# Gates ahead of the last division, logits in two parts, inverse roots on GpSimd, two row turns and four stores moved

## The reference

```
x = x + tanh(g_xattn[0]) * longconv(ctx, ctx, layernorm(x))
x = x + tanh(g_ffn[0])   * routed_lora(layernorm(x))
x = x + tanh(g_xattn[1]) * cross_attention(layernorm(x), ctx)    # 16 heads, int8 fake-quantized projections
x = x + tanh(g_ffn[1])   * moe(layernorm(x))

def layernorm(x): return (x - mean(x)) / sqrt(var(x) + 1e-5)
def moe(x):                                  # 1024 rows of 256
    scores = sigmoid(x @ gate.T)             # 8 experts
    sel = top_k(scores + expert_bias, 2);  s = scores[sel]
    for e in experts: out += silu((s*x) @ w1[e].T) * ((s*x) @ w3[e].T) @ w2[e].T   # rows that chose e
    out += silu(x @ sw1.T) * (x @ sw3.T) @ sw2.T                                    # the shared expert
```

## Time and profile before

| | us |
|---|---|
| median of 3 runs | 219.38 |
| lowest, highest | 218.35, 220.81 |
| the profiled execution | 219.23 |
| its span in the profile | 217.1 |

### The profile page before, as it was taken

The page is one execution under the profiler, slowest core; times in us unless marked ns, Lnnn a source line. Parts: engine busy times, 40 slices in busy tenths (PEclk is TensorE's granted clock), DMA queues, the critical chain, the costliest instruction groups (busy, mean ns, idle before and its releaser), DMA issues.

```text
span 217.1 us, 3560 instructions
## 1 busy us (share of the span) xinstructions
PE 175.5 (81%) x1156; PEld 110.6 (51%) x1156; DVE 167.6 (77%) x465; ACT 101.7 (47%) x256; POOL 81.8 (38%) x114
## 2 busy tenths in 40 slices
PE   0369999989989989885877777887777839989972
PEld 0236555558555556442555556555556417645531
DVE  0798989994178999979889999999957963585634
ACT  2440343211423244642376667776865574553621
POOL 1486557034755540583220204221220195056100
PEclk9999999999999999999599999999999988999998
DMA  6989880000000000000000000000000057456772
GB/s 170 404 232 377 339 268 1 3 0 0 0 0 2 3 2 0 0 0 2 3 0 3 2 0 3 0 3 0 5 0 3 2 97 145 86 97 119 159 170 97
DMA packets 22624, 15.16 MB, mean 70 GB/s; under 512 B 17648, under 2 KB 21328, under 8 KB 22096
## 3 DMA queue, kind: packets, MB, share of 16 engines
q1 hardware_dynamic: 21968, 13.94, 23.4%
q10 hardware_dynamic: 640, 1.02, 1.3%
HBM read 9.68 MB, written 1.07 MB: 50 GB/s over the span
## 4 chain that ended last, share of the span: by engine, by line
PE 40%; DVE 29%; DMA 13%; issue 10%; ACT 3%; SPq 2%; POOL 1%; DVEq 0%; POOLq 0%
DMA R<-R 8%; PE PS L1303 5%; PE PS L1305 5%; PE PS L1304 5%; DVE R L1019 5%; DVE SM L1010 4%; DMA X<-x 4%; PE PS L1391 4%; PE PS L1367 3%; PE PS L1325 3%; PE PS L1630 2%; PE PS L1334 2%; DVE T_R L948 2%; PE PS L1648 2%; PE PS L1579 2%
## 5 line engine op out<-in xcount | busy, mean ns | idle before, releaser
L495 POOL TENSOR_SCALAR R<-QT,SM 128x256 bf16<-128x256 f32 x32 | 16.3, 524 | 26.2 <-DVE SM L1087 19.8
L1256 DVE TENSOR_TENSOR R<-R,PS 128x512 bf16<-128x512 f32 (+1 forms) x17 | 11.7, 686 | 15.8 <-ACT R L761 8.7
L1630 PE MATMUL PS<-R 128*128 128x512 bf16 x64 | 17.5, 395 | 3.5 <-DMA R<-R 3.5
L1010 DVE TENSOR_REDUCE SM<-PS 128x8 f32<-128x1024 f32 x16 | 18.8, 1214 | 1.9 <-PE PS L1454 1.2
L1477 PE MATMUL PS<-CON,R 128*128 128x128 f32 x128 | 19.2, 283 | 1.2 <-ACT R L640 1.2
L471 POOL TENSOR_TENSOR R<-R,CON 128x256 f32<-128x256 f32 x16 | 9.6, 622 | 24.9 <-PE PS L1466 15.7
L640 ACT ACTIVATE R<-PS 128x512 f32<-128x512 f32 x32 | 18.3, 593 | 1.6 <-PE PS L1477 1.4
L1019 DVE TENSOR_TENSOR R<-PS,SM 128x1024 f32<-128x1024 f32 x16 | 18.9, 1215 | 0.0
L336 POOL TENSOR_TENSOR R<-CT 128x512 f32<-128x512 f32 x12 | 13.7, 1142 | 12.5 <-PE PS L1305 7.2
L548 ACT ACTIVATE LNV<-MV,EPSC 128x1 f32<-128x1 f32 (+1 forms) x26 | 7.5, 290 | 22.7 <-DVE MV L933 11.2
L761 ACT ACTIVATE R<-PS 128x512 f32<-128x512 f32 x17 | 10.1, 595 | 14.2 <-PE PS L1630 14.2
(11 more groups left out here) (151 smaller groups left out, 413.0 us busy)
## 6 DMA issues: line engine op xcount, KB each, us to landing
WST<-w SPq DMA_DIRECT2D x3, 1024.0 KB, 11.4
T_R<-lagged SPq DMA_DIRECT2D x2, 768.0 KB, 7.9
X<-x SPq DMA_DIRECT2D x2, 512.0 KB, 6.7
CT<-ctxr SPq DMA_DIRECT2D x1, 1024.0 KB, 7.2
y<-X SPq DMA_DIRECT2D x8, 128.0 KB, 1.9
WKV<-wkv SPq DMA_DIRECT2D x1, 512.0 KB, 9.7
WQP<-wqp ACTq DMA_DIRECT2D x1, 512.0 KB, 6.4
R<-sw SPq DMA_DIRECT2D x3, 128.0 KB, 4.4
```

Of the source, the lines that this page charges most:

```text
L495: nc.gpsimd.tensor_scalar(XB[:, u % XS, j, :], MX[:, b, :], GG[:, b, e:e + 1], 1.0, ALU.mult, ALU.mult).then_inc(e_xb, 1)
L1010: V_.tensor_reduce(MX1[:, b % 2, 8 * c:8 * c + 8], S4[:, 8 * c:8 * c + 8, :], AX.X, ALU.max).then_inc(a_mx, 1)
L1630: ins = M(PS[:, 2 + 2 * (v % 2) + n, :], lhs, rhs, start=(k == 0), stop=(k == NL - 1))
```

## The change

The first group's gates move ahead of block 7's division on VectorE, and block 4's rows behind both. Group 0's logits are made in two parts (three blocks, then the fourth) in another part of bank 6. The gate is a Tanh for both groups now (0.5 tanh(0.5 x) + 0.5, the same sigmoid), so that the addition and the reciprocal go. The inverse roots of blocks 4 to 7 are made by GpSimd, by an addition and a power of -0.5. Block 3's inverse root and rows stand earlier. The transposes of blocks 6 and 7 go from before expert 0 into units 1 and 2. Stores 0 to 3 are issued from ScalarE's queue in units 13 to 16. Group 1's logits and gates move by one unit and in other pieces. The diff without the declarations and a few unchanged lines:

```diff
@@ -318,7 +320,7 @@
         LATE = 3
-        MGT = 2 * GT + 4
+        MGT = 2 * GT + 3
@@ -361,8 +363,9 @@
-        GE_AT = 3
+        GE_AT = 4
+        LOG = 512 - GT * NE
         TC = [0, 2, 4, 10, NH0]
@@ -370,7 +373,7 @@
-            return MGT * (g + 1) - g
+            return MGT * (g + 1)
@@ -424,8 +427,6 @@
                              XB[:, u % XS].rearrange("p j d -> p (j d)"), transpose=True).then_inc(e_td[u % XS], 16)
-                if u >= NG * NE - GT:
-                    store(u - (NG * NE - GT))
             for b in range(GT, NB):
@@ -481,6 +483,13 @@
                 nc.gpsimd.tensor_tensor(X[:, b, :], Y[:, b % 2, :], XPB[:, b, :], ALU.add).then_inc(x3, 1)
+            def late_rstd(b):
+                pool.wait_ge(m_ln, 2 * (b + 1))
+                nc.gpsimd.tensor_scalar(LNV[:, b:b + 1], MV[:, b, 1:2], EPS, None, ALU.add).then_inc(m_rp, 1)
+                pool.wait_ge(m_rp, 2 * (b - GT) + 1)
+                nc.gpsimd.tensor_tensor(RS[:, b:b + 1], LNV[:, b:b + 1], HALFM[:, 0:1], ALU.pow).then_inc(m_rp, 1)
@@ -527,9 +536,15 @@
                 finish(b)
+            late_rstd(GT)
             expert_rows(0)
+            late_rstd(GT + 1)
             expert_rows(1)
-            for u in range(2, NG * NE):
+            expert_rows(2)
+            late_rstd(GT + 2)
+            expert_rows(3)
+            late_rstd(GT + 3)
+            for u in range(4, NG * NE):
                 expert_rows(u)
@@ -678,11 +693,8 @@
                     act.wait_ge(m_gt, gates_done(g - 1))
-                logits = PS[:, 6, 0:GT * NE].rearrange("p (b n) -> p b n", b=GT)
-                if g == 0:
-                    nc.scalar.activation(GE[:, :, :], logits, ACT.Exp, scale=-1.0).then_inc(m_ge, 1)
-                else:
-                    nc.scalar.activation(GE[:, :, :], logits, ACT.Tanh, scale=0.5).then_inc(m_ge, 1)
+                logits = PS[:, 6, LOG:LOG + GT * NE].rearrange("p (b n) -> p b n", b=GT)
+                nc.scalar.activation(GE[:, :, :], logits, ACT.Tanh, scale=0.5).then_inc(m_ge, 1)
@@ -762,34 +774,28 @@
             a_exp(NB - 1, 0)
+            m_rstd(NB - 5)
             o_q_(NB - 3)
             a_exp(NB - 1, 1)
-            m_rstd(NB - 5)
             a_exp(NB - 1, 2)
             o_ev_(NB - 3)
+            m_zt_(NB - 5)
             a_exp(NB - 1, 3)
-            m_zt_(NB - 5)
             o_y_(NB - 3)
             o_pe_(NB - 1)
             o_q_(NB - 2)
-            m_rstd(NB - 4)
+            m_ge_(0)
             o_ev_(NB - 2)
-            m_ge_(0)
             o_y_(NB - 2)
             m_zt_(NB - 4)
+            last_rows(0)
             o_q_(NB - 1)
-            m_rstd(NB - 3)
+            last_rows(1)
             o_ev_(NB - 1)
+            silu(0)
             o_y_(NB - 1)
-            last_rows(0)
-            last_rows(1)
             m_zt_(NB - 3)
-            m_rstd(NB - 2)
-            m_rstd(NB - 1)
-            silu(0)
-            m_zt_(NB - 2)
             last_rows(2)
-            m_zt_(NB - 1)
             last_rows(3)
@@ -799,6 +805,12 @@
                     last_rows(expert(v + XS))
+                if v in (1, 2):
+                    m_zt_(NB - 3 + v)
+                if UNITS - 1 - GT <= v < UNITS - 1:
+                    b = v - (UNITS - 1 - GT)
+                    act.wait_ge(x4, b + 1)
+                    act.dma_start(out[b], X[:, b, :]).then_inc(stored, 16)
             v = UNITS - 1
@@ -1056,7 +1068,10 @@
             def m_rows(b):
-                dve.wait_ge(m_rs, 2 * (b + 1))
+                if b < GT:
+                    dve.wait_ge(m_rs, 2 * (b + 1))
+                else:
+                    dve.wait_ge(m_rp, 2 * (b - GT + 1))
                 V_.tensor_scalar(MX[:, b, :], X[:, b, :], MV[:, b, 0:1], RS[:, b:b + 1], ALU.subtract, ALU.mult
@@ -1064,16 +1079,9 @@
                 s.wait()
-                if k == 0 and g == 1:
+                if k == 1:
                     dve.wait_ge(m_ge, g + 1)
                     s.mark(V_.tensor_scalar(GS[:, :, :], GE[:, :, :], 0.5, 0.5, ALU.mult, ALU.add))
-                elif k == 1 and g == 1:
-                    return
-                elif k == 0:
-                    dve.wait_ge(m_ge, g + 1)
-                    s.mark(V_.tensor_scalar(GE1[:, :, :], GE[:, :, :], 1.0, None, ALU.add))
-                elif k == 1:
-                    s.mark(V_.reciprocal(GS[:, :, :], GE1[:, :, :]))
                 elif k == 2:
@@ -1193,10 +1201,10 @@
-            dve.wait_ge(ones_s, 3)
+            dve.wait_ge(ones_s, 4)
+            m_rows(NB - 5)
             o_norm(NB - 2, 0)
-            m_rows(NB - 5)
             o_norm(NB - 2, 1)
@@ -1204,33 +1212,32 @@
             for k in range(3, 6):
                 o_norm(NB - 2, k)
             finish(NB - 3)
+            m_gates(0, 1)
+            m_gates(0, 2)
+            m_gates(0, 3)
             o_norm(NB - 1, 0)
-            m_rows(NB - 4)
+            m_gates(0, 4)
             o_norm(NB - 1, 1)
-            m_stats(NB - 3, 0)
+            m_gates(0, 5)
             o_norm(NB - 1, 2)
-            m_stats(NB - 3, 1)
+            third_rows(0)
             for k in range(3, 6):
                 o_norm(NB - 1, k)
+            third_rows(1)
+            m_rows(NB - 4)
+            m_stats(NB - 3, 0)
             finish(NB - 2)
+            m_stats(NB - 3, 1)
             m_stats(NB - 2, 0)
-            m_gates(0, 0)
-            m_gates(0, 1)
             m_stats(NB - 2, 1)
-            m_gates(0, 2)
-            m_gates(0, 3)
+            third_rows(2)
+            finish(NB - 1)
             m_rows(NB - 3)
-            m_gates(0, 4)
-            m_gates(0, 5)
-            third_rows(0)
-            third_rows(1)
-            finish(NB - 1)
             m_stats(NB - 1, 0)
             m_stats(NB - 1, 1)
+            third_rows(3)
             m_rows(NB - 2)
-            third_rows(2)
             m_rows(NB - 1)
-            third_rows(3)
             for v in range(UNITS):
@@ -1255,9 +1262,12 @@
-                if GE_AT < v <= GE_AT + 3:
-                    m_gates(1, 2 * (v - GE_AT - 1))
-                    m_gates(1, 2 * (v - GE_AT - 1) + 1)
+                if v == GE_AT + 1:
+                    for k in range(1, 4):
+                        m_gates(1, k)
+                if v == GE_AT + 2:
+                    for k in range(4, 6):
+                        m_gates(1, k)
                 if v >= 1 and (v + XS) % (NE + 1) and v + XS < UNITS:
@@ -1570,15 +1580,17 @@
-            def m_logits(g):
+            def m_logits(g, lo, hi):
                 if g == 0:
                     pe.wait_ge(L["gate"], 16)
-                pe.wait_ge(m_zt, GT * (g + 1))
-                for j in range(GT):
+                pe.wait_ge(m_zt, GT * g + hi)
+                for j in range(lo, hi):
                     for k in range(NL):
-                        ins = M(PS[:, 6, NE * j:NE * j + NE], MZT[:, g, k, P * j:P * j + P], GW[:, k, :],
+                        at = LOG + NE * j
+                        ins = M(PS[:, 6, at:at + NE], MZT[:, g, k, P * j:P * j + P], GW[:, k, :],
                                 start=(k == 0), stop=(k == NL - 1))
-                ins.then_inc(m_gl, 1)
+                if hi == GT:
+                    ins.then_inc(m_gl, 1)
@@ -1660,6 +1672,7 @@
             o_rows(NB - 2)
+            m_logits(0, 0, GT - 1)
             o_transpose(NB - 3)
@@ -1667,9 +1680,9 @@
                 a_values(NB - 1, k)
+            m_logits(0, GT - 1, GT)
             o_transpose(NB - 2)
             o_rows(NB - 1)
-            m_logits(0)
             o_project(NB - 2)
@@ -1677,9 +1690,7 @@
             m_transpose(NB - 3)
-            m_transpose(NB - 2)
             e_hidden(1, 0)
-            m_transpose(NB - 1)
             e_hidden(1, 1)
@@ -1687,8 +1698,10 @@
                 e_out(v - 1)
+                if v in (1, 2):
+                    m_transpose(NB - 3 + v)
                 if v == GE_AT - 1:
-                    m_logits(1)
+                    m_logits(1, 0, GT)
```

5 lines of the change are left out of this document (4 added, 1 removed).

## The result

The changed kernel takes 224.3 us (median of 4 runs, 222.97 to 224.62). Beside it the kernel before took 220.09 (median of 4, 218.35 to 222.32). The ratio is 1.0175, with a 95% interval of 1.0127 to 1.0223: longer, clear of the noise, though the interval does not say whether by more or less than 2%. Ratios here leave out the executions that fell in the chip's slower state, medians and spreads keep them. The forecast was 220.2 with a range of 217.6 to 222.0, which is no clear change, so the measured time lies outside the range. The chain that it described (the stall ahead of block 4's transpose, the low clock, block 7's chain) is there; several of its terms were mis-sized, all to the same side.

What follows compares the result with a forecast made beforehand. It took the chain of waits to bound the tail: GpSimd's rows and a DMA transpose before expert 0, then TensorE, last the sync queue. 219.23 + 2.05 (front, with clock) - 1.0 (stores) = 220.3, stated as 220.2; range 217.6 to 222.0.

Steps and rivals of the forecast that it cites:

- Part 1: Group 0's gates: written at 170.2 instead of 173.0, 2.8 us earlier, with a new 1.28 us table load before the Tanh.
- Part 2: Work behind the gates: block 4's rows end at 172.0, 4.5 us later; expert 0 starts at 178.8 against 177.89.
- The clock's term: TensorE's clock falls in a 3.2 us stall before block 4's transpose; shared expert's first half and transpose take 1.2 us longer.
- The rival "the clock stays up": TensorE's stall before block 4's transpose, 3.2 us against 3.9, does not lower the clock: 219.1 us; chance 0.27.
- Part 3: Inverse roots by power on GpSimd: 0.3 us per power, between 0.2 and 0.75; expert 1 at 182.8 instead of 182.37.
- +0.35 for block 7's transpose: On TensorE, block 7's transpose, formerly in the shadow of the wait, now stands between two experts: 0.35 us later.
- +0.1 for group 1's gates: On VectorE, the second group's gates run in two pieces ahead of the product of unit 6: 0.1 us later.
- The rival with a slow power: Powers of 0.75 us each in block 7's chain add 0.5, and a second clock fall is near: 222.0 us; chance 0.13.
- Part 4: Four stores leave the sync queue among the last transposes: gain of 1.0 us, between 0.3 and 1.8.
- The sign that I had named: At the end, the last four transposes standing 1.3 to 1.5 us apart would show the prediction right.

Runs made afterwards that it cites:

- the run with a busy TensorE: Changed kernel plus twelve bf16 products (128x512) into an unused PSUM bank ahead of block 4's transpose: median 224.33 us, ratio 1.0112; profiled run 220.23.
- Twelve small products: Twelve 32-column TensorE products added ahead of block 4's transpose to the kernel of four changed orders: 216.05 us, ratio 0.982.
- four changed orders: Changed kernel with block 4's rows before the gates, block 7's y before the first Silu, unit 0's product before blocks 6 and 7's rows, stores last: 215.84 us.

## Why the prediction was wrong

**The gates (Part 1)** came as forecast: Tanh at 168.1 net, gates at 170.2, 2.8 earlier. The load cost 1.28, with 0.01 behind it. The drain that the Trainium skill (ScalarE: Activation LUTs, What ACT_TABLE_LOAD costs) adds to each switch of tables isn't seen at either load here.

**What stands behind them (Part 2)** was right in its mechanism. Block 4's rows ended at 172.2 net (forecast 172.0), and expert 0 waited for block 5's transpose and not for a DMA, through the links that were listed. It began 2.97 later than before, where the forecast had 0.9 and 1.2 for the clock. **The clock's term was mis-sized**: I doubled a part of the shared expert's first half; the whole of it, 1.88 to 3.62, and block 4's transpose (0.48 to the next instead of 0.23) ran at 1.2 GHz (the granted clock is 0.50 there). That is 1.9 instead of 1.2, and the run with a busy TensorE gave 1.8. The rival "the clock stays up" rested on the stall being shorter than the one before; the clock fell inside it (0.79 in 172 to 173, 0.50 in 173 to 174).

**The power (Part 3)** was mis-sized too: 0.58 (0.56 to 0.72 in all) where I took 0.3, though the row of 0.73 was there as the upper bound. From block 7's statistics to the inverse root it took 0.97 instead of 0.55, and the multiplication in its place gave 0.37 back. With the 0.9 that expert 0's chain had already lost, the output of unit 0 began 3.15 later than before where the sum had 1.7. From there on the +0.35 for block 7's transpose and the +0.1 for group 1's gates are not seen: expert 1 is at +2.83, no later than the output. No run tested these two terms. The rival with a slow power had its mechanism half right: the price was there; the second fall of the clock is not in the changed kernel's profile, but in those of two variants with the same wait of 1.27.

**The stores (Part 4) were the step that failed**: 1.0 forecast, 0 measured, in three comparisons (the changed kernel with the one before, with its own stores put back, and the store edit alone). The trace of before pointed at the reason with the share of the DMA engines, 0.89 of 8 us, and I used it only for one end of the range and took the middle. After the change it is 0.97. The Trainium skill (DMA: Bandwidth & Descriptors, Rules for kernel authors) says that more queues bring no bandwidth. The traces agree: the last transposes left 1.4 apart and the last two took 4.1 to 4.8 to land, in the changed kernel and with the store edit alone. The sign that I had named, a spacing of 1.3 to 1.5, came true without the gain; it looked at the issue and not at the landing.

**The eighth transpose** was in no term: it landed after 4.8 instead of 3.1, of which 0.6 to 0.7 reach the end by the profiles.

Together, against a forecast tail of +1.05 (2.05 less 1.0): +1.0 for the front, about what the clock (0.7) and the power (0.4) were short, +0.7 for the eighth transpose and +1.0 for the stores make 3.75 of the 3.77. So three of the parts were off to the same side, each within or near its own bounds, and the range had allowed one or two of them at a time. Another 0.9 of the miss lies in the base: the sum started from one execution of 219.23, while the median of the kernel before was 220.09 beside the changed one. The changed kernel's profiled execution lies a further 1.73 higher by a spell of low clock near 100 us that the change doesn't touch (two slices at 5 on its page, one in the earlier trace rows).

What the change wanted is not wrong. Once block 4's rows, block 7's y and unit 0's product are moved ahead of what held them up, its front is the better one: with the stores behind the last transpose in each, the tail is 60.79 with the old front and 57.01 to 58.85 with the new one. The other parts of the change (the logits in two parts, block 3's earlier root, the transposes of blocks 6 and 7 in later units, group 1's gates) were in every variant of it and have no price of their own.

## What to carry to other kernels

When a result is made earlier on an in-order engine, list what is now queued behind it and behind each of those; here the gates came 2.8 earlier and expert 0, behind what they had been put ahead of, 3.0 later. Where the DMA engines of a stretch are near full, a transfer moved to another queue may gain nothing (here 0); move it out of the stretch (here 1.3). A stall that may lower TensorE's clock should be priced with all the work that follows in that spell at half the speed, not with part of it.

## What the runs showed of the hardware

**A fetch of instructions can hold up a DMA transpose.** In seven traces a packet of the instruction queue came about 2.65 to 2.85 us behind the issue of the eighth transpose, and this landed after 4.7 to 4.9. In six it came 3.1 to 3.7 behind, and the transpose landed after 3.1. In one kernel the fetch fell 0.6 behind the issue of the seventh, which landed after 3.5 instead of 3.1. Twelve small products moved the packet and the delay went with it. That rests on one moved packet and the thirteen other traces. How the fetch does it I don't know: the packet is 16 KB and takes 0.9 to 1.3 us in the fourteen traces, and the landing was 1.7 later.

**The clock after short stalls.** In a stall of 3.36 to 3.37 the clock fell to 1.2 GHz in each of five profiles. Two waits of 1.48 and 1.27 around expert 0, with about 1 us of work between them, were followed by a fall in two profiles. Waits of 1.16 and 1.27 (the changed kernel) and even of 1.73 and 1.26 (with the products in the earlier stall) were not. Behind waits of 1.3 and 0.46 around block 7's rounding it fell in one profile (four changed orders, granted clock 0.62 in 174 to 178) and not in the three others that have the same two waits. Nothing in these runs says which short waits are safe.

**The power** of a 128x1 tile on GpSimd takes 0.71 to 0.72 the first time and 0.56 to 0.58 after that; a multiplication of the same shape 0.34 the first time and 0.19 to 0.22 after that, so each power is 0.36 to 0.38 longer. An addition of a constant takes 0.21 to 0.23.
